# Graph attention on one core: x arrives also transposed and GpSimd splits it, instead of TensorE transposes and splits out of PSUM

## What is computed

```
q, k, v = heads(x @ Wq), heads(x @ Wk), heads(x @ Wv)        # 8 heads of 32
scores  = q k^T / sqrt(32), masked with adj
out     = softmax(scores) v
x       = layernorm(x + relu(out) @ Wo)                      # attention stage
y       = x
for l in range(3):                                           # the later layers
    y = layernorm(y + additive_attention(y, adj))
    y = layernorm(y + gelu(y @ W1 + b1) @ W2 + b2)
out     = layernorm(x + y)
```

## Time and profile before

| | |
|---|---|
| median of 3 runs | 1895.09 us (1894.74 to 1895.41) |
| span of the profiled execution | 1892.0 us |
| that execution's own device time | not given apart from the runs; span and median differ by 3.1 us |
| instructions | 40139 |
| TensorE busy | 1672.9 us (88%) |
| VectorE busy | 1513.0 us (80%) |
| ScalarE busy | 1120.7 us (59%) |
| GpSimd busy | 1314.4 us (69%) |
| attention stage | up to about 422 us of the span |

### The profile page before, as it was taken

How to read it: one execution, slowest core, us unless ns; L and a number is a source line. 1 busy time by engine, 2 the same in 40 slices (tenths; PEclk the granted TensorE clock), 3 DMA queues, 4 the chain that set the end, 5 groups by cost and what they waited for, 6 DMA issues and landing times.

```text
span 1892.0 us, 40139 instructions
## 1 busy us (share of the span) xinstructions
PE 1672.9 (88%) x12032; PEld 1482.6 (78%) x12032; DVE 1513.0 (80%) x5366; ACT 1120.7 (59%) x2718; POOL 1314.4 (69%) x1690
## 2 busy tenths in 40 slices
PE   5999999965999999999899999999989898989895
PEld 4777777754888888888788888888878787878784
DVE  3888888877788778788887887887888888888873
ACT  3888888864556556556465565565554545554542
POOL 3355555534787787787777877877868787888786
PEclk8999999996999999999899999999999898999998
DMA  5233333323121121121211211211212122212101
GB/s 181 63 89 89 89 89 89 89 79 123 34 67 58 42 67 58 42 67 54 91 56 44 67 52 47 67 53 47 67 34 68 64 70 65 68 64 69 63 26 45
DMA packets 150477, 127.31 MB, mean 67 GB/s; under 512 B 14880, under 2 KB 143392, under 8 KB 150432
## 3 DMA queue, kind: packets, MB, share of 16 engines
q1 hardware_dynamic: 145024, 124.30, 21.4%
q10 hardware_dynamic: 5408, 2.50, 0.5%
HBM read 89.03 MB, written 37.75 MB: 67 GB/s over the span
## 4 chain that ended last, share of the span: by engine, by line
PE 24%; DVE 20%; POOL 19%; issue 11%; ACT 3%; POOLq 1%; DVEq 0%; ACTq 0%
PE ps L45 14%; PE ps L819 6%; POOL gnn_norm L154 5%; DVE gnn_junk L913 5%; PE ps L795 3%; DVE gnn_small L929 2%; POOL gnn_norm L742 2%; POOL gnn_h L746 2%; POOL xo L761 2%; POOL gnn_norm L757 2%; POOL inv L149 2%; DVE gnn_small L934 2%; DVE gnn_small L937 2%; DVE gnn_res L972 1%; DVE gnn_st L976 1%
## 5 line engine op out<-in xcount | busy, mean ns | idle before, releaser
L819 PE MATMUL ps<-gnn_w_hi,gnn_g_hi 128*128 128x256 f32 x1536 | 454.8, 296 | 41.7 <-DVE gnn_res L972 41.0
L819 PE MATMUL ps<-gnn_w_lo,gnn_g_hi 128*128 128x256 f32 x1536 | 445.7, 290 | 0.0
L819 PE MATMUL ps<-gnn_w_hi,gnn_g_lo 128*128 128x256 f32 x1536 | 444.9, 290 | 0.0
L141 POOL TENSOR_TENSOR fence_pool<-half_neg 128x1 f32<-128x1 f32 x304 | 64.1, 213 | 477.3 <-DVE gnn_mv L1063 169.0
L980 DVE TENSOR_TENSOR gnn_g_lo<-ps,gnn_g_hi 128x512 fp32r<-128x512 f32 x384 | 263.1, 685 | 135.3 <-ACT ps L893 135.2
L892 ACT ACTIVATE gnn_g_hi<-ps,b_cols 128x512 fp32r<-128x512 f32 x384 | 264.5, 689 | 179.4 <-PE ps L45 155.3
L819 PEld LDWEIGHTS ps<-gnn_w_hi,gnn_g_hi 128*128 128x128 f32 x1536 | 305.6, 199 | 47.5 <-DVE gnn_res L972 44.8
L45 PE MATMUL ps<-gnn_hT_hi,gnn_w_hi 128*128 128x512 f32 x768 | 333.4, 434 | 4.0 <-DVE gnn_g_lo L980 4.0
L869 ACT ACTIVATE gnn_e<-gnn_u,gnn_small 128x128 f32<-128x128 f32 x192 | 74.9, 390 | 400.3 <-DVE gnn_small L938 400.3
L819 PEld LDWEIGHTS ps<-gnn_w_lo,gnn_g_hi 128*128 128x128 f32 x1536 | 306.7, 200 | 1.9
L819 PEld LDWEIGHTS ps<-gnn_w_hi,gnn_g_lo 128*128 128x128 f32 x1536 | 305.8, 199 | 0.0
(11 more groups left out here) (116 smaller groups left out, 3925.2 us busy)
## 6 DMA issues: line engine op xcount, KB each, us to landing
hist<-xo SPq DMA_DIRECT2D x48, 512.0 KB, 3.3
x<-hist SPq DMA_DIRECT2D x48, 512.0 KB, 4.3
gmask<-mask_hist SPq DMA_DIRECT2D x48, 256.0 KB, 4.5
aw<-in_L_gnn_attn_w SPq DMA_DIRECT2D x48, 256.0 KB, 4.3
att_xq<-in_x SPq DMA_DIRECT2D x16, 512.0 KB, 4.8
att_xl<-in_x SPq DMA_DIRECT2D x16, 512.0 KB, 3.5
gnn_fin<-hist SPq DMA_DIRECT2D x16, 512.0 KB, 3.8
out<-gnn_fin SPq DMA_DIRECT2D x16, 512.0 KB, 2.8
```

Of the source, the lines that this page charges most:

```text
L141: e.tensor_tensor(fence_pool[:, n:n + 1], half_neg[:, 0:1], half_neg[:, 0:1], ALU.add)
L819: mm = e.matmul(FF2[j % 2], g[a][:, m, j * N:(j + 1) * N], V[b][:, m, :], start=(n == 0), stop=(n == len(terms) - 1))
```

## The change

The host also hands over `xT`: for each step the array [128, 1024], whose partition is a feature (of 128) and whose columns are 2 halves of the features by 512 nodes. SyncE loads it to `xT_raw` in place of `xq`. GpSimd makes the high part by four copies of 128x256 with rounding and the low part by four subtractions of 128x256, all from SBUF. TensorE's eight transposes per step, ScalarE's two copies and VectorE's two subtractions are gone. GpSimd does step t + 2's split behind its masks of step t + 1 and ahead of its layernorm of step t, once the six projections of step t + 1 are made.

```diff
@@ sync
+                def load_xT(t):
+                    e.dma_start(xT_raw[:].rearrange("p k n -> p (k n)"),
+                                xT_in[bass.ds(t, 1)].rearrange("o p n -> p (o n)")).then_inc(xT_ld, 16)
-                e.dma_start(xq[:], block_of(x_g, 0)).then_inc(xq_ld, 16)
+                load_xT(0)
...
-                e.wait_ge(xT_made, 2)
-                e.dma_start(xq[:], block_of(x_g, 1)).then_inc(xq_ld, 16)
+                e.wait_ge(xT_lo_out, 1)
+                load_xT(1)
...
-                        e.wait_ge(xT_made, 2 * (t + 2))
-                        e.dma_start(xq[:], block_of(x_g, t + 2)).then_inc(xq_ld, 16)
+                        e.wait_ge(xT_lo_out, t + 2)
+                        load_xT(t + 2)
@@ gpsimd
+                PARTS = [(k, slice(n * TOK // 2, (n + 1) * TOK // 2)) for k in range(KT) for n in range(2)]
+
+                def split_xT(t1):
+
+                    hold_pool(e, xT_ld, 16 * (t1 + 1))
+                    if not isinstance(t1, int) or t1:
+                        hold_pool(e, proj_made, 6 * t1)
+                    for k, half in PARTS:
+                        ins = e.tensor_copy(xT[0][:, k, half], xT_raw[:, k, half])
+                    ins.then_inc(xT_hi_out, 1)
+                    e.wait_ge(xT_hi_out, t1 + 1)
+                    for k, half in PARTS:
+                        ins = e.tensor_tensor(xT[1][:, k, half], xT_raw[:, k, half], xT[0][:, k, half].bitcast(F32),
+                                              ALU.subtract)
+                    ins.then_inc(xT_lo_out, 1)
+
+                split_xT(0)
                 make_masks(0, 0, 0)
+                split_xT(1)
...
+                    if a2:
+                        split_xT(t + 2)
@@ tensor
-                def transpose_x(t1, k):
...
                     if n == 0 and 0 in parts:
-                        e.wait_ge(xT_hi_out, 2 * (t1 + 1))
-                        e.wait_ge(xT_lo_out, 2 * (t1 + 1))
-                    if n >= 2 and 0 in parts:
+                        e.wait_ge(xT_lo_out, t1 + 1)
+                    if 0 in parts and (n >= 2 or not isinstance(t1, int) or t1):
                         e.wait_ge(proj_out, 6 * t1 + n - 1)
...
-                    if j == 3 and half == 0 and a2:
-                        for k in parts:
-                            transpose_x(t + 2, k)
@@ scalar
-                def xT_hi(t1, k):
-                    e.wait_ge(xT_made, 2 * t1 + k + 1)
-                    e.copy(xT[0][:, k, :], A[k]).then_inc(xT_hi_out, 1)
...
-                for k in range(KT):
-                    xT_hi(0, k)
@@ vector
-                def xT_lo(t1):
-                    for k in range(KT):
-                        e.wait_ge(xT_hi_out, 2 * t1 + k + 1)
-                        e.tensor_tensor(xT[1][:, k, :], A[k], xT[0][:, k, :].bitcast(F32), ALU.subtract).then_inc(xT_lo_out, 1)
```

More of the change, by code:

```diff
@@ L194, in gnn_kernel @@
             wa_ld = sems("wqk_ld", "wvo_ld")
[L195 removed]
+            wa_split, xT_ld = sems("wa_split", "xT_ld")
             x_ld = sems("x_ld_even", "x_ld_odd")
[L197 removed]
+            (masks_made, xT_hi_out, xT_lo_out, proj_made, proj_out, s_made, scored, peaked, exped,
              pT_made, pT_out_b, pT_out_a, pv_made, den_inv, rden_out, rdenT_made, rdenT_out, att_out,
              attT_hi_out, attT_lo_out, wo_made, y_out, bn_out, eye_made, eye_added) = sems(
[L200 removed]
+                "masks_made", "xT_hi_out", "xT_lo_out", "proj_made", "proj_out", "s_made", "scored",
                 "peaked", "exped", "pT_made", "pT_out_b", "pT_out_a", "pv_made", "den_inv", "rden_out",
@@ L320, in _ @@
                 e.wait_ge(ident_set, 1)
-                def transpose_x(t1, k):
-                    if k == 0:
-                        e.wait_ge(xq_ld, 16 * (t1 + 1))
-                    if not isinstance(t1, int) or t1:
-                        e.wait_ge(proj_out, 6 * t1 - 1 + k)
-                    for j in range(GROUP):
-                        mm = e.transpose(A[k][:, j * N:(j + 1) * N], xq[:, j, k * P:(k + 1) * P], ident[:])
-                    mm.then_inc(xT_made, 1)
                 def project(t1, par, n, parts=(0, 1)):
@@ L453, in body @@
                         e.copy(probsT[:, 4:8, :].rearrange("p h n -> p (h n)"), PB[1]).then_inc(pT_out_b, 1)
-                        if j == 3 and a2:
-                            for k in range(KT):
-                                xT_hi(t + 2, k)
                         if has1 and j < 3:
@@ L478, in _ @@
                     proj_copy(0, 0, n)
-                for k in range(KT):
-                    xT_hi(1, k)
                 e.wait_ge(peaked, 1)
@@ L544, in body @@
                             statistics(i - 1, 1 - par, GROUP - 1)
-                        if j == 3 and a2:
-                            xT_lo(t + 2)
                         e.wait_ge(rdenT_out, START + i + 1)
@@ L573, in _ @@
                 split_weights(0)
-                xT_lo(0)
                 split_weights(1)
                 masked_scores(0, 0, 0, 0)
-                xT_lo(1)
                 masked_scores(1, 0, 0, 1)
@@ L1106 @@
     arrays, args = {}, []
+    x = np.asarray(inputs["x"])
+    B, N, D = x.shape
+    laid = dict(inputs)
+    laid["xT"] = (x.reshape(B // GROUP, GROUP, N, D // P, P).transpose(0, 4, 3, 1, 2)
+                  .reshape(B // GROUP, P, D // P * GROUP * N))
+    names.insert(1, "xT")
     for name in names:
-        a = np.ascontiguousarray(inputs[name])
+        a = np.ascontiguousarray(laid[name])
         arrays[f"in_{name}"] = a
```

9 lines of the change are left out of this document (2 added, 7 removed).

## The result

| | before | after |
|---|---|---|
| median of 20 runs each | 1893.79 us (1892.05 to 1895.49) | 1898.1 us (1894.15 to 1901.35) |
| the profiled execution: time, span | span 1892.0 us | 1896.97 us, span 1895.0 us |
| instructions | 40139 | 39923 |
| VectorE busy | 1513.0 us | 1503.7 us (79%) |
| ScalarE busy | 1120.7 us | 1105.5 us (58%) |

The ratio is 1.0023, with a 95% interval of 1.0017 to 1.003: a little slower, at the edge of the 0.2% that can be told from no change. The forecast was 1897.5. The time came out nearly right; two terms of the sum did not, and they largely cancelled.

A forecast was written before the change was run, and what follows sets the result against it. No single engine bounds the attention stage; the engines work in a ring. Collisions net of the saving +6.2, start -4.3 and one-time cost +0.5 give +2.4 on 1895.09: 1897.5 us, range 1886 to 1904.

The forecast's parts named there:

- the collisions: Graph j = 3: GpSimd's split holds up VectorE's L539, L553 and L555, 0.8 us a step (0 to 1.75).
- L553 and L555 at their old lengths: Sign against the forecast: VectorE's high and low part in graph j = 3 not lengthened; 0.2 and 0.45 us were expected.
- The saving of 0.36 us a step from step 14's graph: VectorE's path in graph j = 3 shortens to that of step 14, which prepares no x: 5.0 us over 14 steps.
- The subtraction at 0.74 us: GpSimd's price for one 128x256 subtraction of the split, from a line through two trace rows.
- The copy at 0.57 us: GpSimd's price for one 128x256 rounding copy of the split, with bounds of 0.37 and 0.97 us.
- TensorE's removed work at nothing: Graph j = 3: dropping TensorE's eight transposes saves nothing more, since it waits for VectorE's low part (L555) either way.
- The start at -4.3 us: ScalarE issues the constants' loads 5.55 us sooner, less a 1.28 us table load: gain 4.3 us, bounds 0 and 5.55.
- the one-off cost of 0.5: At the start, step 1's split and the L303 addition now run beside VectorE's first graph: 0 to 1.8 us, taken as 0.5.
- Rival A: The collisions in graph j = 3 do not bite: 8.8 us gained, 1886.3 us, faster; chance 0.20.
- Rival B: GpSimd's split ends too late for TensorE, 0.3 to 0.5 us a step more: about 1903 us; chance 0.10.
- Rival C: The start does not move, as the element-wise loads take until about 24 us anyway: 1901.8 us, slower; chance 0.12.
- Rival D: The collisions in graph j = 3 are half the size: 1891.9 us; chance 0.08.

The follow-up runs named there:

- placed: Kernel after, two of GpSimd's subtractions moved to run once L528 of graph j = 3 is done, two behind VectorE's low part: 1886.09 us, ratio 0.996.

## Why the prediction was right, and where it was not

The forecast of 1897.5 us and its sign were right, and for the closeness luck did much. The sum was +2.4 us, on a median of three runs that was 1.3 us above that of twenty; between the medians it is +4.3 and between the spans +3.0. In it the collisions are put 3.7 us too high, and the clock, 5.5 us, is missing; that step 15 came out 1.1 us shorter is chance. By its own sign, "L553 and L555 at their old lengths, would prove me wrong", it was wrong about where the split collides: both kept their lengths. By its steps:

- **The saving of 0.36 us a step from step 14's graph: right.** With nothing in VectorE's way graph j = 3 takes 5.67 us (placed), 0.34 less than before.
- **The subtraction at 0.74 us: right** (0.73). **The copy at 0.57 us: wrong**, 0.40, near the lower bound of 0.37. This one price moved the collisions to other instructions.
- **The collisions at 0.8 us a step: the mechanism was right, the place and the size were not.** The prediction had L539 (now L528) beside the copies, at 0.15, and L553 and L555 beside the subtractions, at 0.2 and 0.45. With the faster copies the first subtraction starts 0.06 us before L528 and holds it by 0.52, and the split is over as the high part begins, so that the other two cost nothing. 0.52 in place of 0.8, or 14 x (0.52 - 0.36), 2.2 us by its sum and 2.5 measured, in place of 6.2. The kernel with the later subtractions shows that the other two holds exist, with 0.69 us.
- **GpSimd's copies as a cause: right in kind, at no cost here.** In the kernel after the copies end before L528 begins. With pieces of 128 columns L528 meets one, and is held until 0.15 us before its end, as by a subtraction; that costs 0.03 us, because the copy is nearly over. What a copy costs when it is met at its beginning was not tried.
- **TensorE's removed work at nothing: wrong**, and the largest error. "TensorE in j = 3 waits for VectorE's low part of the attention (L555) either way" is true of the order of the work and leaves out the clock. Its waits grew from 1.10 to 1.82 us, the clock fell behind some steps, and that costs 5.5 us in the profiled execution. Neither the loss of the transposes alone (placed: none) nor the hold alone (the kernel before with the split: none) does it; both together do.
- **The start at -4.3 us: right at the first copy** (-4.38), of which 3.65 arrive, so that the one-off cost of 0.5 was 0.73. It was not taken apart further, and the start's scatter is larger than it. The size came out in part by luck. The prediction let the last three loads take as long as before; they began 12.31 - 5.77 = 6.54 us sooner, not 5.55, and took 0.88 longer, and in the kernel with the held loads they took 10.30.
- **The later layers at nothing: right** (-0.26, within their scatter).
- **Rival A**, no collisions, 1886.3, is what the placed kernel gives (1886.09): the rival's gain was real, behind a condition on the order that the change did not meet. **Rival B** fell with the copy's price; the low part was never late for TensorE. **Rival C** fell at -4.38. **Rival D** is nearest for the collisions by themselves and would have given 1891.9, too low by the clock's part.

The Trainium skill ("SBUF — State Buffer", "Who interferes with whom") has the shared port pair as an exclusive lock for a whole instruction. For the subtractions the runs agree: the hold follows their length at 256 and at 512 columns (the copy of 1/sum takes 0.81 and 1.01 us), down to the last 0.15 us. For the copies of 128 columns they agree in the same way, and for the instructions that make the masks only in part (last section).

## What to carry to other kernels

Work moved to an idle engine was not free here, though that engine had room: lay its start and end beside the neighbour's instructions, one by one, and place it by a wait where the neighbour waits for a third engine. That was worth 12 us here, where piece sizes only moved the cost about. When a change takes work away from TensorE, add up its waits in that stretch before and after, and look at the granted clock of each step, not at its mean. Compare the profiled executions stage by stage as well: here the start and the untouched layers scattered by 2.5 and 3.7 us, about as much as the change's whole effect (4.3 us). And test a by-product, such as the place of a DMA in a queue, on the old kernel too.

## What was not expected of the hardware

- The granted clock fell to 0.50 behind graph j = 3 in one to four of 14 steps in the kernels whose TensorE waits there summed to 1.74 to 2.09 us, and in none with 0.84 to 1.41. What decides which steps are hit stays open.
- A hold does not depend only on the kind of GpSimd instruction. The earlier trace rows show a high part of 0.30 us beside a compare; in the kernel after the same pair, met later in the compare, reads (GpSimd, then VectorE):

```profile
69.34 1.95 POOL L294 TENSOR_SCALAR att_mask<-att_adjl 128x512 f32<-128x512 int32 x1
...
70.71 0.73 DVE L540 CAST att_attT_hi<-att_att 128x256 fp32r<-128x256 f32 x1
```

  Begun 1.37 us behind the compare's start, and not 0.89 as there, the high part takes 0.73 us; 70.71 + 0.73 - 0.29 = 71.15 is again some 0.15 us before the end, 71.29. The traces of the fourteen kernels have 793 cases of VectorE's copy of 1/sum, high part or low part begun inside one of GpSimd's two mask instructions of 512 columns, 1.93 to 1.95 us long. All 15 begun in its first 0.37 us are held until 0.46 us behind its start. None of the 632 begun between 0.6 and 1.3 us is held. Of the 146 begun later four are, the only high parts among them, begun at 1.36 to 1.39 us and held until 1.80; the 139 low parts are not. So such an instruction holds at its beginning and towards its end, and not between. Why is open.
- Three element-wise loads of constants kept their queue for 12.33, 13.21, 10.30 and, on SyncE's queue, 6.40 us. Something beside the loads themselves sets this time; what it is was not tried.
